# dt by one Softplus, the mask's matmuls as four 64x64 quadrants, and the softmax reciprocals widened by ScalarE and turned by transposes

## The reference

```python
# Mamba branch
xz = x @ in_proj_w.T;  x_inner, z = split(xz)                  # 512 channels each
x_conv = silu(causal_conv4(x_inner) + conv_b)
dt_lr, B, C = split(x_conv @ x_proj_w.T)                        # 16, 16, 16 columns
dt = softplus(dt_lr @ dt_proj_w.T + dt_proj_b)
dA = exp(dt * A);  dBx = dt * x_conv * B                        # A = -exp(A_log), 16 states
h = dA * h + dBx;  y = sum_states(h * C)                        # scan over the tokens
out = (y + x_conv * D) * silu(z) @ out_proj_w.T
# attention layer, two times; window 128, 8 heads of 64
h = shift_token(x);  q, k, v = split(h @ wqkv)
q, k = rotary_xpos(l2norm(q) * qs, l2norm(k) * ks)
sim = (8 * q) @ [k_previous, k_own].T;  sim = where(mask, -max, sim)
x = x + (softmax(sim) @ [v_previous, v_own]) @ wo
h = layernorm(shift_token(x)) @ w1 + b1;  a, g = split(h)
x = x + (a * gelu(g)) @ w2 + b2
```

## Time and profile before

| | us |
|---|---|
| median of 3 runs | 2244.7 (2244.4 to 2245.45) |
| the profiled execution, its own time | 2240.71 |
| its span in the profile | 2238.9 |
| TensorE busy, share | 2058.0, 92% |
| VectorE busy, share | 2016.8, 90% |
| ScalarE busy, share | 1680.9, 75% |
| GpSimd busy, share | 928.2, 41% |

### The profile page before, as it was taken

One profiled execution on the slowest core, in us unless ns is written; L12 is line 12 of the kernel. 1 busy time (PEld: TensorE's weight loads), 2 busy tenths in 40 slices (PEclk: granted clock), 3 DMA queues, 4 the chain that ended last, 5 costly groups with the idle time before them and its releaser, 6 DMA issues. The chain is left out here.

```text
span 2238.9 us, 37820 instructions
## 1 busy us (share of the span) xinstructions
PE 2058.0 (92%) x10944; PEld 1318.1 (59%) x10944; DVE 2016.8 (90%) x2804; ACT 1680.9 (75%) x4087; POOL 928.2 (41%) x1086
## 2 busy tenths in 40 slices
PE   6789989999899999999899998999989999898897
PEld 2355666656566566665566565666556656565565
DVE  2999989999899999999899998999989999899893
ACT  3777877968778787887778777787777868778682
POOL 2444343444434444443444433444443443533440
PEclk9889999999999999999999999999999999999999
DMA  4567767686676756877756876668667686667482
GB/s 142 145 152 194 188 155 183 180 205 175 161 196 178 188 161 157 220 187 169 193 136 189 208 187 165 157 179 200 181 166 196 173 197 167 163 162 217 115 200 54
DMA packets 113131, 388.52 MB, mean 174 GB/s; under 512 B 11408, under 2 KB 32272, under 8 KB 94368
## 3 DMA queue, kind: packets, MB, share of 16 engines
q0 software_dynamic: 46080, 151.02, 36.0%
q1 hardware_dynamic: 66848, 235.10, 31.4%
HBM read 238.75 MB, written 155.71 MB: 176 GB/s over the span
## 5 line engine op out<-in xcount | busy, mean ns | idle before, releaser
L756 DVE TENSOR_TENSOR_SCAN hb<-dA,state,hb 128x512 f32<-128x512 f32 x512 | 668.3, 1305 | 34.7 <-ACT dA L963 20.5
L1177 POOL COPY state<-hb 128x2 f32<-128x2 f32 x256 | 223.5, 873 | 638.5 <-DVE hb L756 638.2
L963 ACT ACTIVATE dA<-dt_sb,amat 128x512 f32<-128x512 f32 x512 | 344.3, 720 | 81.8 <-DMA ysum<-dA 80.8
L1193 POOL DMA_DIRECT2D ysum<-dA x256 | 220.2, 883 | 382.6 <-DVE dA L763 272.6
L1465 PE MATMUL ring<-hT,w 128*128 128x256 f32 (+1 forms) x1536 | 354.5, 388 | 17.4 <-ACT hT L1119 16.9
L1465 PEld LDWEIGHTS ring<-hT,w 128*128 128x128 f32 (+1 forms) x1536 | 272.6, 182 | 94.5 <-ACT hT L1119 26.0
L749 DVE TENSOR_TENSOR hb<-u_sb,bc 128x1024 f32<-128x1024 f32 x256 | 311.3, 1216 | 2.0 <-DMA bc<-bc_rows 1.9
L763 DVE TENSOR_TENSOR dA<-hb,bc 128x1024 f32<-128x1024 f32 x256 | 307.2, 1200 | 0.0
L1073 ACT ACTIVATE rot<-rot,rnorm 128x64 f32<-128x64 f32 x1024 | 257.2, 339 | 50.8 <-POOL rnorm L1262 50.7
L1098 ACT ACTIVATE probs<-ring,nmax 128x256 f32<-128x256 f32 x512 | 235.6, 483 | 55.5 <-DVE nmax L847 55.1
L1262 POOL TENSOR_TENSOR rnorm<-rnorm,powers 128x8 f32<-128x8 f32 x128 | 230.2, 1799 | 23.5 <-POOL rnorm L1259 23.5
(11 more groups left out here) (122 smaller groups left out, 3469.8 us busy)
## 6 DMA issues: line engine op xcount, KB each, us to landing
bc<-bc_rows SPq DMA_DIRECT2D x128, 1024.0 KB, 5.8
ysum<-dA POOLq DMA_DIRECT2D x256, 512.0 KB, 7.2
wqkv<-in_wqkv SPq DMA_DIRECT2D x48, 512.0 KB, 8.6
w<-in_w SPq DMA_DIRECT2D x16, 1364.0 KB, 9.5
w<-in_w SPq DMA_DIRECT2D x16, 768.0 KB, 10.7
tab<-in_tab SPq DMA_DIRECT2D x64, 128.0 KB, 5.7
wo<-in_wo SPq DMA_DIRECT2D x16, 512.0 KB, 10.0
ysum<-xconv POOLq DMA_DIRECT2D x32, 256.0 KB, 5.1
```

Source lines behind the costliest of these rows:

```text
L756: dve.tensor_tensor_scan(hb[:, k % H_RING, :], dA[:, k % DA_RING, :], hb[:, k % H_RING, :], state[:, k:k + 1], ALU.mult, ALU.add).then_inc ...
L963: act.activation(dA[:, k % DA_RING, :], dt_sb[:, j, :], ACT.Exp, scale=amat[:, n:n + 1]).then_inc(dA_ready.sem, 1)
```

## The change

Three edits, with new lists of stages for all engines.

1. dt is one Softplus on ScalarE, from PSUM with the bias; clip and max are gone from VectorE, and Identity, Exp, Ln from ScalarE.
2. The identity is kept as two 64x64 blocks, and the mask as [two halves of the query rows] by 512 columns on both halves of the partitions. Each call of `scores` makes four matmuls of 64 rows and 64 columns: for each half of the query rows one into each of the two banks.
3. After the reciprocal ScalarE writes it 64 times side by side into `rb` (`widen`), TensorE transposes `rb` in four 128x128 blocks, and ScalarE copies the bank back over `rb`.

Beside them, -exp(A_log) is computed in place, and the mask is loaded by one DMA instead of two.

```diff
-            def clip(half):
-                ...
-                    dve.tensor_scalar(u_sb[:, j, :], dt_sb[:, j, :], 40.0, None, ALU.min).then_inc(dtmin_ready.sem, 1)
-
             def u(half):
 
-                for j in range(half * JH, half * JH + JH):
-                    dve.wait_ge(*dtlog_ready.at(it, j + 1))
-                    dve.tensor_tensor(dt_sb[:, j, :], dt_sb[:, j, :], u_sb[:, j, :], ALU.max)\
-                       .then_inc(dt_ready.sem, 1)
                 for j in range(half * JH, half * JH + JH):
                     dve.wait_ge(*dt_ready.at(it, j + 1))
                     dve.wait_ge(*xconv_ready.at(it, j + 1))
+                    dve.wait_ge(*dBx_ready.at(it - 1, (half + 1) * SUMS // HALVES))
                     dve.tensor_tensor(u_sb[:, j, :], dt_sb[:, j, :], xconv[:, j, :], ALU.mult).then_inc(u_ready.sem, 1)
@@
             def invert(a):
                 dve.wait_ge(*probs_ready.at(it, (a + 1) * HEADS))
-                dve.wait_ge(*filled(it if a else it - 1, ("rb", (a - 1) % NA)))
+                dve.wait_ge(*widened.at(it, a))
                 dve.reciprocal(rinv[:, :], rowsum[:, :]).then_inc(rinv_ready.sem, 1)
@@
-            def dt_out(j):
+            def softplus(j):
                 act.wait_ge(*filled(it, ("dt", j)))
                 act.wait_ge(*dA_ready.at(it - 1, (j // JH + 1) * UNITS // HALVES))
-                act.activation(dt_sb[:, j, :], bank(it, ("dt", j))[:, :], ACT.Identity,
-                               bias=par[:, C_DTB + j:C_DTB + j + 1]).then_inc(dtv_ready.sem, 1)
-
-            def softplus(half):
-                ...
+                act.activation(dt_sb[:, j, :], bank(it, ("dt", j))[:, :], ACT.Softplus,
+                               bias=par[:, C_DTB + j:C_DTB + j + 1]).then_inc(dt_ready.sem, 1)
@@
+            def widen(a):
+
+                act.wait_ge(*rinv_ready.at(it, a + 1))
+                act.wait_ge(*oT_ready.at(it, a))
+                act.activation(rb[:, :, :].rearrange("p a (h d) -> p (a h) d", h=2),
+                               rinv[:, :].unsqueeze(2).to_broadcast([P, HEADS, DH]), ACT.Copy).then_inc(widened.sem, 1)
+
             def rb_out(a):
                 act.wait_ge(*filled(it, ("rb", a)))
-                act.wait_ge(*oT_ready.at(it, a))
                 act.activation(rb[:, :, :], bank(it, ("rb", a))[:, :].rearrange("p (a t) -> p a t", a=NJ), ACT.Copy)\
@@ scores
-                msk = mask0[:, :] if it == 0 and w == 0 else mask[:, w % 2, :]
+                first = 2 * WIN if it == 0 and w == 0 else w % 2 * WIN
                 for p in (2 * c, 2 * c + 1):
                     pe.wait_ge(*freed(it, ("s", a, p)))
-                    pe.matmul(bank(it, ("s", a, p))[:, :].rearrange("p (h k) -> p h k", h=2), identb[:, :],
-                              msk.unsqueeze(1).to_broadcast([P, 2, 2 * WIN]), start=True, stop=False,
-                              skip_group_check=True)
+                for part in range(2):
+                    for odd in range(2):
+                        rows = slice(odd * DH, (odd + 1) * DH)
+                        out = bank(it, ("s", a, 2 * c + odd))[part * DH:(part + 1) * DH, :]
+                        pe.matmul(out.rearrange("p (h k) -> p h k", h=2), identb[rows, :],
+                                  mask[rows, part, first:first + 2 * WIN].unsqueeze(1).to_broadcast([DH, 2, 2 * WIN]),
+                                  start=True, stop=False, skip_group_check=True)
@@
             def spread(a):
-                pe.wait_ge(*rinv_ready.at(it, a + 1))
+
+                pe.wait_ge(*widened.at(it, a + 1))
                 pe.wait_ge(*freed(it, ("rb", a)))
-                for h in range(HEADS):
-                    g, odd = divmod(h, 2)
-                    m = pe.matmul(bank(it, ("rb", a))[odd * DH:(odd + 1) * DH, g * WIN:(g + 1) * WIN],
-                                  rinv[:, h:h + 1].to_broadcast([P, DH]), ident[:, :], start=True, stop=True)
-                m.then_inc(*done(it, ("rb", a)))
+                flip(("rb", a), [rb[:, g, :] for g in range(PAIRS)])
```

The lists keep every other stage and change their order. Of the first pass, to the first `pT` or scan, these are the new ones:

```diff
 PE_FIRST
-xnT(0) xnT(1) in(0) in(1) in(2) in(3) conv(0) conv(1) conv(2) conv(3) q(0) xdbl dt(0) dt(1) k(0) heads(0)
-s(0,0) s(0,1) pT(0,0) v(0) pT(0,1) k(1) pT(0,2) pT(0,3) q(1) o(0,0) o(0,1) o(0,2) z(0) rb(0) o(0,3) z(1)
+xnT(0) q(0) xnT(1) k(0) in(0) in(1) in(2) in(3) conv(0) conv(1) conv(2) conv(3) heads(0) xdbl q(1) dt(0)
+dt(1) v(0) s(0,0) s(0,1) k(1) z(0) z(1) z(2) z(3) heads(1) q(2) pT(0,0) pT(0,1) pT(0,2) k(2) o(0,0) o(0,1)
 DVE_FIRST
-norm(0) norm(1) +norm(0) turn(q,0) dt(0) +norm(1) turn(k,0) u(0) scan scan m(0,0) m(0,1) m(0,2) m(0,3) scan
+norm(0) norm(1) turn(q,0) turn(k,0) turn(q,1) +norm(0) u(0) m(0,0) m(0,1) m(0,2) m(0,3) scan scan scan
```

More of the change, by code:

```diff
@@ L91 @@
[L91 to L100, removed]
++scan +scan w2(2) o(6) m(7,0) m(7,1) m(7,2) m(7,3) +scan +scan rinv(7) +turn(q,0) +turn(k,0) o(7) wo(6)
@@ L101 @@
++m(6,1) +m(6,2) +m(6,3) +scan +scan +turn(q,7) +scan +h(2,0) ++u(0) +h(2,1) +turn(k,7) +rinv(6) +h(2,2)
++scan +h(2,3) +h(2,4) +h(2,5) +scan +scan
 """
 ACT_ORDER = """
-+dA heads(7) +dA v(7) e(7,0) e(7,1) e(7,2) e(7,3) +q(0) pT(7,0) pT(7,1) pT(7,2) pT(7,3) +k(0) +dA rb(7)
-+turn(q,0) +turn(k,0) +v(0) +heads(0) +dA +dA +q(1) hn(3) +e(0,0) +e(0,1) +pT(0,0) +k(1) +e(0,2) +e(0,3)
-last(3) hT(3) +dt(2) +dA +dA +dt(3) +dA +dA +dA h(3,0) h(3,1) h(3,2) +turn(q,1) h(3,3) h(3,4) h(3,5) +rb(0)
-+start(0) +dA +dA +turn(k,1) +dA +dA +pT(0,1) +pT(0,2) +softplus(1) +dA +pT(0,3) +heads(1) +dA +dA +z(0)
@@ L120 @@
+++dt(0) ++dt(1) +dA +dA +e(5,0) +e(5,1) +rb(4) +e(5,2) +e(5,3) +v(5) +q(6) +k(6) +rinv(5) +pT(5,0) +pT(5,1)
++dA +dA +pT(5,2) +dA +pT(5,3) +turn(q,6) +rb(5) +turn(k,6) +dA +dA +v(6) +heads(6) +e(6,0) +e(6,1) +hn(2)
++q(7) +hT(2) +e(6,2) +e(6,3) +k(7) +pT(6,0) +dA +dA +h(2,0) +h(2,1) +last(2) +h(2,2) +turn(q,7) ++skip(0)
++rinv(6) +pT(6,1) +h(2,3) +h(2,4) +h(2,5) +pT(6,2) +dA +dA ++dA +rb(6) +pT(6,3) +turn(k,7) ++dA
 """
 POOL_ORDER = """
-add(30) add(31) scan +scan merge(1) +turn(q,0) +turn(k,0) +scan +q(1) +add(0) +add(1) stats(3) +skip(0)
@@ new lines @@
++turn(k,3) +add(10) +scan +carry ++norm(0) +add(11) ++norm(1) +scan +add(12) +add(13) +scan +scan +add(14)
++q(4) +add(15) +scan +add(16) +add(17) +scan +turn(q,4) +turn(k,4) +skip(1) +scan +scan +stats(1) +add(18)
++add(19) +q(5) +scan +scan +turn(q,5) +add(20) +add(21) +merge(0) +scan +add(22) +scan +turn(k,5) ++tail
++scan +add(23) +q(6) +add(24) +add(25) +scan +turn(q,6) +scan +turn(k,6) +scan +add(26) +add(27) +stats(2)
++scan +q(7) +scan +turn(q,7) +add(28) +add(29) +turn(k,7) +scan ++q(0) +carry2
@@ L150 @@
+w2(2)
 """
 DVE_FIRST = """
[L152 to L156 removed]
@@ L179 @@
+turn(k,6) dA heads(6) last(2) dA dA dA e(6,0) e(6,1) e(6,2) q(7) dA dA e(6,3) k(7) hn(2) v(6) pT(6,0)
+pT(6,1) rinv(6) hT(2) pT(6,2) h(2,0) h(2,1) pT(6,3) dA dA h(2,2) h(2,3) h(2,4) h(2,5) dA dA turn(q,7)
+turn(k,7) +dA rb(6) +skip(0) +dA
 """
 POOL_FIRST = """
-halo norm(0) norm(1) q(0) turn(q,0) turn(k,0) +norm(0) scan scan q(1) add(0) add(1) turn(q,1) turn(k,1) scan
-skip(0) scan scan q(2) add(2) add(3) add(4) scan turn(q,2) turn(k,2) add(5) scan scan add(6) +norm(1) scan
-scan q(3) add(7) add(8) turn(q,3) turn(k,3) add(9) stats(0) carry scan add(10) scan add(11) tail scan scan
@@ new lines @@
+scan add(7) q(3) stats(0) scan carry +halo scan add(8) add(9) scan turn(q,3) turn(k,3) add(10) scan scan
+add(11) add(12) add(13) scan scan scan q(4) add(14) add(15) scan scan add(16) add(17) turn(q,4) turn(k,4)
+scan skip(1) stats(1) scan q(5) scan add(18) add(19) turn(q,5) add(20) turn(k,5) add(21) scan +tail scan
+scan add(22) add(23) q(6) merge(0) scan scan add(24) add(25) turn(q,6) turn(k,6) q(7) scan stats(2) add(26)
+scan add(27) scan turn(q,7) add(28) turn(k,7) add(29) scan carry2 +q(0) scan
```

341 lines of the change are left out of this document (161 added, 180 removed).

## The result

The changed kernel takes 2212.2 us against 2244.6: the median of runs of 2213.8, 2212.2 and 2204.1, without a fourth of 2877 at a mean clock of 0.65 (with that one the median is 2213.0, the value that the expectations below use). The ratio is 0.985, 95% interval 0.982 to 0.988: 1.5% faster, where 1.8% was forecast. The profiled execution has a span of 2211.9 us, 27.0 less than before.

A forecast was written before the change was run, and what follows sets the result against it. VectorE and TensorE, both nearly full, bound the kernel, VectorE's saving being the smaller. 35 + 3 (start) + 2 (waits) = 40 less from 2240.7 gives 2200.7; with the median 4.0 higher, 2205 us, 8-in-10 range 2188 to 2234.

The forecast's parts named there:

- the mask: TensorE's mask call: four quadrants at once take 0.33 us instead of 0.52, 24 us less over 128 calls.
- the reciprocals: TensorE: four 128x128 transposes replace eight fp32 matmuls per window, 36 us less; bounds 30 and 42.
- Rivals (a) and (c): Mask quadrants on TensorE: only pairs overlap, 2212, chance 0.12; or they run one behind the other, 2260, chance 0.06.
- the estimate of 0.39: Mask call in us if the skill's mode-change drain applies: 0.21 + 0.18, saving 17 us instead of 24.
- 35.0 us go: VectorE: removing clip and max of dt takes off 35.0 us, 4.4 a chunk; bounds 37.6 and 30.
- The smaller of the two savings is the measure: VectorE and TensorE both nearly full: a gain counts fully only if both get it; VectorE's 4.4 a chunk against 7.5.
- Waits: VectorE's waits shrink through new slack on TensorE: 0.3 us in seven chunks, 2 us; bounds 15 less, 20 more.
- The half I named: VectorE's wait for scores from TensorE, 4.3 of the middle stretch's 9.5 us of waits; some were to go.
- the 13: Sign of being wrong: VectorE's waits in a middle stretch of 270 us exceed 13 us.
- ScalarE and the widening: ScalarE: about 11 us less in sum, of no weight with 58 idle us per stretch; widening priced at nothing in steady chunks.
- Rival (b): New order buys back waits: VectorE's grow by 3 us a chunk, 24 of the 40 go: 2229; chance 0.12.
- Start and end: Second scan at 66 where 70.19 stood, 3 us less, bounds 0 and 8; last window nothing, rest of tail unchanged.

The follow-up runs named there:

- Runs 1 to 3: Rotary-table product cut to 1 of 64 columns in kernel before (2235.7 us), in changed kernel (2202.7 us); moved from GpSimd to VectorE in changed kernel (2220.4 us).
- Runs 4 and 11: Changed kernel with the mask back to two 128x128 matmuls (2223.1 us); changed kernel with the reciprocals back to eight fp32 matmuls a window (2222.6 us).
- rinv_only: Kernel before, its lists kept, with only the widened reciprocals, the widening some five stages ahead of rb: 2282.5 us, ratio 1.0162.
- sp_only: Kernel before, its lists kept, with only the Softplus edit, dt(2) moved next to dt(3) on ScalarE: 2271.1 us, ratio 1.0108.
- light_after: Changed kernel with GpSimd multiplying only 1 of 64 columns of each rotary table: 2202.7 us, ratio 0.9796.

## Why the prediction was right in size, and which steps failed

**TensorE, right for the mask, a little high for the reciprocals.** 24 + 36 less was forecast, with busy time near 1990; measured are 0.34 us a call (forecast 0.33) and 2003.0 in all. The flips take 42.3 us where a quarter of 142.1, 35.5, had been worked out, so the reciprocals save 29.5, just under the lower bound of 30. The clock has no part in the 55 (76.5 and 74.8 us of the busy time at 1.2 GHz). Rivals (a) and (c) fall with the 0.34. The Trainium skill, "TensorEngine Tiling (Array Packing)", section Tiling Modes, has the drain at a change of mode and no figure for it; the estimate of 0.39 that was put beside its rule is 0.05 too long.

**VectorE, wrong by 25 of 35 us.** The step said that 35.0 us go, with a lower bound of 30 for port contention "that another instruction now meets". The mechanism was named and its size was taken from the max alone. I did not look at where the new lists put GpSimd's table product. They doubled the stretching of the scans and products (19.2 to 45.1 us), and VectorE lost 10.2.

**"The smaller of the two savings is the measure", wrong.** This step carried the forecast. By it, with VectorE's measured 10.2, the time would be 15 us less, 2230. It was 32.4 less. Runs 1 to 3 show it: 22, 41 and 21 us off VectorE's work gave 12, 11 and nothing. Runs 4 and 11 show it for TensorE: 19 and 23 us more busy time cost 7 each (best values; zero and some 16 are not excluded). I read this as two engines at 91% that hand work back and forth through fixed lists and are held by the lists more than by either one's work. That reading is argued, not shown: the periods of runs 4 and 11, 2.3 and 3.0 us longer for 2.4 and 2.8 us a chunk of TensorE work, would also fit a TensorE that sets the pace of the middle chunks and is hidden at the end, and one execution of each can't tell. That the size came out is luck, two errors of opposite sign: less VectorE work went than was written, and more waits went with it.

**Waits, wrong by size and in the reason.** 2 us were put down, with bounds of 15 less and 20 more; 16.8 less idle time came, just past the bound. The half I named is the one that went (scores, 41.6 to 6.3), but 36.9 us of new waits, for the B and C rows and GpSimd's state, and 18.7 more for ScalarE's squares came with it, which I had not looked for. And the reason, TensorE's slack, is not the one: with all three edits in the lists of before and TensorE 19 us lighter the wait for scores is 51.3, with the new lists and none of the edits 9.4. The new order removed it. In the middle stretch VectorE's waits are 10.7 us together against 9.5, below the 13 that I had set as a limit, and made of other parts:

```profile
DVE hb L744 <- DMA bc<-bc_rows: 4.5, 1, 4.5
DVE hb L744 <- POOL state L1159: 2.4, 2, 1.7
...
DVE nmax L833 <- PE ring L1382: 0.2, 1, 0.2
```

**ScalarE and the widening, right only for the new lists.** 130 loads, 684 ns for a Softplus (0.69) and 624 for a widening (0.61) are as forecast, and the page after shows no cost. But the reason I gave, 58 idle us in the stretch, does not hold the weight: `rinv_only` has ScalarE idle for the same quarter and pays 36 us, `sp_only` pays 26 for its loads. Rival (b), waits that come back by the longer path, is what happens in the kernels with the old lists and the widening. That the change escapes it is the work of its lists, and the step should have priced them instead of the stages in them.

**Start and end.** The second scan was forecast near 66 and runs at 64.1; the third is the one that waits now, until 71.2, where the kernel before made its third at 72.7. So the start gave 1.5 us by then, not 3 (first pair, then the wait):

```profile
62.87 2.46 DVE L751 TENSOR_TENSOR_SCAN hb<-dA,state,hb 128x512 f32<-128x512 f32 x2
...
71.05 0.20 DVE L840 RECIPROCAL rinv<-rowsum 128x8 f32<-128x8 f32 x1 [1.95 <-ACT probs L1074]
71.17 1.27 DVE L751 TENSOR_TENSOR_SCAN hb<-dA,state,hb 128x512 f32<-128x512 f32 x1
```

The first chunk, from scan 0 to scan 64, went from 245.7 to 236.0 us, 9.8 less with 4.4 of dt's work in it. The six next ones went from 268.7 to 265.6 each, where 263 was forecast, 18.7 together. The tail stayed (318.6 and 319.5), as said, though its last product waits 7.22 us for the head outputs where 4.51 stood in the earlier trace rows.

What stays open: which of the many moved stages in the new lists earns the 4.2 points between 1.0272 and 0.9847, and how much a list laid out for one edit alone would give. No run separates it. Nor does any run take time off the DMAs or the rest of GpSimd's work, though ScalarE's waits moved there too: for the DMAs that read the ring of dA 80.8 us before and 54.3 after, for GpSimd's `rnorm` 50.7 and 89.2.

## What to carry to other kernels

When every engine's order is written out by hand, operations and order are one thing: an edit timed in the old lists measures the lists' misfit (here +1.1% and +1.6% for edits that take 29 and 19 us of work away), and a new list timed with the old operations does too. Forecast such a change by where each moved or new stage makes another engine wait, not by the busy time it saves; two engines at 91% are no proof that either sets the pace. Before crediting work taken off VectorE, look at what GpSimd will then stand beside, and do not write off the table loads of ScalarE as idle time used: in the old lists 42 us of them cost 26.

## What the runs showed of the hardware

GpSimd's 128x256 product of two SBUF operands stretches a VectorE scan from 1.28 to as much as 2.59 us and a product from 1.20 to 2.09 (the rows above), and is itself stretched from 0.72 to 2.37; beside reads of PSUM or a one-operand reduce both keep their length. With 4 instead of 256 elements per partition the same GpSimd instruction takes 0.20 us alone. Of 85 scans and products that it overlaps in `light_after` none is stretched; the GpSimd instruction is, to 0.70 on average and 1.56 at most (spans on that engine are rough). One that starts within a scan ends with it, at 970.32 (VectorE, then GpSimd, `light_after`):

```profile
969.03 1.29 DVE L751 TENSOR_TENSOR_SCAN hb<-dA,state,hb 128x512 f32<-128x512 f32 x1
```

```profile
969.48 0.84 POOL L1230 TENSOR_TENSOR tabs<-tab,qks 128x4 f32<-128x4 f32 x1
```

The Trainium skill, "SBUF — State Buffer", section "SBUF: two separate sides", says that VectorE with two SBUF inputs and a GpSimd operation that reads SBUF lock the shared port pair against each other: the one that starts first has it for the whole instruction, the other blocks. Which pairs collide agrees with these traces, and so do these two rows. The full-size pair above does not: the scan of 972.19 starts before the product of 972.65 and still loses 1.31 us, more than the product's whole 1.04.

A load of another table took 1283 ns in each of the 120 to 155 cases of a kernel here. Taking 33 of them away took 40.7 us off ScalarE's busy time, 1.23 each, and 26 us off the time. The Trainium skill, "ScalarE: Activation LUTs", section "What ACT_TABLE_LOAD costs", gives the load the same 1283 ns and adds a drain, 2.66 us per switch in all. No drain shows here: over the 155 loads of `sp_only` the median gap to the instruction before is 18 ns and to the one after 12 ns.

Four bf16 quadrants of 64x64 with 512 columns, over two PSUM banks, take 0.34 us at the full clock against 0.52 for two matmuls of 128x128 that write the same elements, and 0.57 against 0.96 at 1.2 GHz.
